# Summing the products of a state-space scan in pairs on GpSimd before TensorE sums over the states

## What is computed

```python
def step(state, inp):
    u, dlt, Bs, Cs = inp
    dA = jnp.exp(dlt.reshape(b, NC, DPG)[..., None] * A_g)
    du = (dlt * u).reshape(b, NC, DPG)
    state = dA * state + du[..., None] * Bs[:, :, None, :]
    y = jnp.einsum('bgdn,bgn->bgd', state, Cs).reshape(b, D_INNER)
    return (state, y)
_, ys = jax.lax.scan(step, init, (u_t, d_t, B_t, C_t))
```

## Time and profile before

| | |
|---|---|
| median of 3 runs | 2097.96 us (2095.51 to 2100.2) |
| the profiled execution | 2099.33 us, its span 2097.5 us |
| PE busy | 1651.5 us, 79% |
| DVE busy | 1770.0 us, 84% |
| ACT busy | 1035.9 us, 49% |
| POOL busy | 913.8 us, 44% |
| mean granted TensorE clock | 0.899 |

### The profile page before, as it was taken

How to read it: one execution, slowest core, us unless ns; L and a number is a source line. 1 busy time by engine, 2 the same in 40 slices (tenths; PEclk the granted TensorE clock), 3 DMA queues, 4 the chain that set the end, 5 groups by cost and what they waited for, 6 DMA issues and landing times. The chain is left out here.

```text
span 2097.5 us, 22567 instructions
## 1 busy us (share of the span) xinstructions
PE 1651.5 (79%) x5875; PEld 725.3 (35%) x5948; DVE 1770.0 (84%) x3142; ACT 1035.9 (49%) x1745; POOL 913.8 (44%) x676
## 2 busy tenths in 40 slices
PE   3375577778996889868997799878997899779856
PEld 1122123232452335322452335332452335234324
DVE  6577899989879998979989998999989987987830
ACT  3247444825555454735556355734547344734312
POOL 0101534454437434554346434464346544665510
PEclk9977699979997999979997899979997899999978
DMA  4100222222222222222231222222222223223300
GB/s 108 46 0 21 72 79 89 92 69 77 75 92 65 85 71 86 85 67 78 74 101 65 81 76 76 96 75 72 76 96 71 76 85 106 86 99 113 110 10 11
DMA packets 94601, 157.95 MB, mean 75 GB/s; under 512 B 10940, under 2 KB 23660, under 8 KB 94468
## 3 DMA queue, kind: packets, MB, share of 16 engines
q1 hardware_dynamic: 94468, 156.43, 22.9%
HBM read 143.83 MB, written 12.58 MB: 75 GB/s over the span
## 5 line engine op out<-in xcount | busy, mean ns | idle before, releaser
L1226 POOL TENSOR_TENSOR prod<-state,c_all 128x512 f32<-128x512 f32 x512 | 669.6, 1312 | 706.8 <-DVE state L1203 644.0
L1203 DVE TENSOR_TENSOR_SCAN state<-decay,ps_b 128x512 f32<-128x512 f32 x512 | 619.7, 1210 | 9.7 <-issue 0.4
L750 PE MATMUL ps_y<-prod,idf 128*128 128x512 f32 x1024 | 610.6, 689 | 4.8 <-DVE u L1216 3.6
L1210 DVE TENSOR_TENSOR ps_b<-du,ps_b 128x512 f32<-128x512 f32 x512 | 347.7, 679 | 87.3 <-PE ps_b L743 86.8
L919 ACT ACTIVATE decay<-delta,a_neg 128x512 f32<-128x512 f32 x512 | 359.3, 719 | 32.3 <-DVE state L1203 29.3
L743 PE MATMUL ps_b<-b_rows,sel_b 48*128 48x512 bf16 x512 | 209.9, 411 | 155.0 <-DVE state L1203 152.7
L750 PEld LDWEIGHTS ps_y<-prod,idf 128*128 128x128 f32 x1024 | 183.8, 207 | 136.3 <-issue 109.9
L743 PEld LDWEIGHTS ps_b<-b_rows,sel_b 48*128 48x128 bf16 x512 | 47.8, 94 | 467.3 <-DVE state L1203 332.5
L619 PE MATMUL ps_x<-xT,w 128*128 128x512 bf16 (+1 forms) x391 | 132.0, 422 | 80.1 <-DVE arena_l L1095 65.6
L826 ACT ACTIVATE arena_l<-ps_x 128x512 f32<-128x512 f32 (+1 forms) x104 | 61.8, 594 | 190.8 <-PE ps_x L619 189.7
L535 PE MATMUL ps_x<-hT,win 128*128 128x512 bf16 (+1 forms) x455 | 135.6, 441 | 21.4 <-DVE arena_b L1171 16.6
(11 more groups left out here) (230 smaller groups left out, 2422.2 us busy)
## 6 DMA issues: line engine op xcount, KB each, us to landing
c_all<-c_rows SPq DMA_DIRECT2D x512, 256.0 KB
c_rows<-arena_l SPq DMA_DIRECT2D x32, 256.0 KB
out<-arena_b SPq DMA_DIRECT2D x8, 512.0 KB
x_in<-in_base SPq DMA_DIRECT2D x8, 256.0 KB
c_all<-in_winT SPq DMA_DIRECT2D x1, 1280.0 KB, 7.5
arena_b<-in_w_fc SPq DMA_DIRECT2D x1, 1024.0 KB, 5.7
arena_b<-in_w_proj SPq DMA_DIRECT2D x1, 1024.0 KB, 5.0
w<-in_w1T SPq DMA_DIRECT2D x1, 792.0 KB, 5.9
```

What stands on the lines that cost most here:

```text
L750: nc.tensor.matmul(ps_y[:], idf[:], prod[:, n % NP, :], start=(n % NST == 0), stop=(n % NST == NST - 1)).then_inc(reduced, 1)
L1203: nc.vector.tensor_tensor_scan(state[:, n % NS, :], decay[:, n % NDA, :], ps_b[:, n % NDB, :], 0.0, ALU.mult, ALU.add).then_inc(scanned, 1)
L1210: nc.vector.tensor_tensor(ps_b[:, j % NDB, :], du[:, slot(s, ct), :], ps_b[:, j % NDB, :], ALU.mult).then_inc(driven, 1)
L1226: nc.gpsimd.tensor_tensor(prod[:, n % NP, :], state[:, n % NS, :], c_all[:, n % NC, :], ALU.mult).then_inc(multiplied, 1)
```

## The change

POOL, after an odd product n, waits for its own product and adds it into the even one before it (new line L1228; the products are L1224 there). A new semaphore `paired` goes up by 2 with each add. PE makes one matmul for a pair instead of one for each product (L752 there), in the slot of the odd one (n + 3), and raises `reduced` by 2. `sums_at` goes. The even product now waits for the matmul of the pair four and three before it, the odd one for the add of that pair. In all 512 sums on PE become 256, and POOL gets 256 adds of 128 x 512 f32, all operands in SBUF.

```diff
             if part == 2:
-                for n in sums_at(j):
-                    if n % NST == 0:
-                        wait(eng, y_taken, s.count(PER, n))
-                    eng.wait_ge(multiplied, s.count(PER, n + 1))
-                    nc.tensor.matmul(ps_y[:], idf[:], prod[:, n % NP, :], start=(n % NST == 0),
-                                     stop=(n % NST == NST - 1)).then_inc(reduced, 1)
-
-        def sums_at(j):
-
-            n = j - 3
-            if not 0 <= n < PER or n % NST == 0:
-                return []
-            return [n - 1, n] if n % NST == 1 else [n]
+                n = j - 3
+                if 0 <= n < PER and n % 2 == 1:
+                    if n % NST == 1:
+                        wait(eng, y_taken, s.count(PER, n - 1))
+                    eng.wait_ge(paired, s.count(PER, n + 1))
+                    nc.tensor.matmul(ps_y[:], idf[:], prod[:, (n - 1) % NP, :], start=(n % NST == 1),
+                                     stop=(n % NST == NST - 1)).then_inc(reduced, 2)
...
                 eng.wait_ge(c_spread[n % 8], s.count(2 * PER, 16 * (n // 8 + 1)))
-                wait(eng, reduced, s.count(PER, n + 1 - NP))
+                if n % 2 == 0:
+                    wait(eng, reduced, s.count(PER, n + 2 - NP))
+                else:
+                    wait(eng, paired, s.count(PER, n + 1 - NP))
                 eng.wait_ge(scanned, s.count(PER, n + 1))
                 nc.gpsimd.tensor_tensor(prod[:, n % NP, :], state[:, n % NS, :], c_all[:, n % NC, :],
                                         ALU.mult).then_inc(multiplied, 1)
+                if n % 2 == 1:
+                    eng.wait_ge(multiplied, s.count(PER, n + 1))
+                    nc.gpsimd.tensor_tensor(prod[:, (n - 1) % NP, :], prod[:, (n - 1) % NP, :], prod[:, n % NP, :],
+                                            ALU.add).then_inc(paired, 2)
```

More of the change, by code:

```diff
@@ L442, in sandwich @@
         multiplied = sem("multiplied")
+        paired = sem("paired")
         reduced = sem("reduced")
```

## The result

The changed kernel takes **2125.4 us** (median of 4 runs, 2123.85 to 2129.3), the one before 2098.07 us beside it. The ratio is 1.0132, with a 95% interval of 1.0117 to 1.0146: slower by 28 us, where 14 us less was forecast. The time lies almost on rival A's, but as the runs show, not by A's sum.

The account below looks back on a forecast made before the run. The prediction took DVE to bound most of a sequence and PE some stretches. Its terms, -61 + 41 + 3 + 3 = -14 us, gave 2084 us, with a range of 2054 to 2126.

Parts of the forecast that it names:

- rival A: DVE stands still longer than PE's relief is worth: 82 us uncovered, +5 for late roots, -61; 2124 us, chance 0.33.
- What bounds the kernel: DVE nearest to full, 1578 of 1746 us busy; PE the bound in some stretches of each sequence.
- term 1: Half of PE's sums go: 0.53 of DVE's 115.6 us of waits at L1210 and the norm comes back, -61 us.
- term 3: Later POOL results delay DVE by +3 us (0 to 20); PE's wait for the add counted as hidden.
- term 2: POOL's 256 adds make DVE instructions with SBUF operands stand still: 58 us, of which +41 us remains after cover.
- term 4: With less work PE may be granted a lower clock, delaying first matmuls of a burst: +3 us (0 to 15).
- made it a rival: Rival B: relief and standing still cancel, or the longest PE waits stand behind other lines' matmuls; 2098 us, chance 0.14.
- L1216 unchanged: DVE's 28.3 us of waits at L1216 for a block's last sums stay, within 10 us over eight ends; counted as 0.
- step that hides an add behind the product: PE's sum waits for POOL's product and add, 2.6 us, but its slot comes 3.8 us later at the shortest: hidden.
- the 0.88 that I had given as a mark: Sign against term 4: a mean PE clock well under 0.88 would break it.
- C's large form: POOL late in middle sequences too, 0.5 us for each of 200 pairs: about 2190 us; chance 0.05 with other slower outcomes.

Follow-up runs that it names:

- relief_selected: Kernel before with only 70 of its sums removed, for selected pairs of products, and no adds (those odd products not summed): 2064.0 us, ratio 0.9841 to the kernel before.
- relief: Changed kernel with half the sums but without the adds on POOL (odd products not summed): 2061.5 us, ratio 0.9836 to the kernel before.
- adds_all_sums: Changed kernel with its adds but 512 sum matmuls on PE again: 2156.8 us, ratio 1.0286 to the kernel before.
- small_pow: Changed kernel with each add on POOL replaced by a power of 128x6, all waits kept: 2076.8 us, ratio 0.9909 to the kernel before.
- tail_pow: Changed kernel with only the adds of states 52 to 63 replaced by a power of 128x6: 2114.9 us, ratio 1.0088 to the kernel before.

## Why the prediction was wrong, by its steps

**What bounds the kernel: right.** DVE bounds most of a sequence, PE two stretches of it and the last feed-forward.

The forecast was 42 us too low (-14 against +28). By the runs, 27 of them are term 1, 12 term 3 and 6 term 2, less the 3 of term 4, whose size is not measured apart: it is inside the relief as the runs show it.

**Term 1, the relief (-61, measured -34): the term that was most mis-sized, and the step that failed.** The stretches were the right ones, but the share 0.53 of 115.6 us was carried over to all sequences from half of the sums' time in a window. *relief_selected* shows that the sums of the stretches where PE is the bound are worth as much as all. In *relief* the two waits fell from 115.6 to 74.3 us, a share of 0.36, and DVE became 8 us more busy (1770.0 to 1778.4), which I had not priced; together a share of 0.29 came back. Part of the base could not shrink: a wait of 4.1 us in each of the second to sixth sequences stands in every one of these kernels at its old length, behind projections and the Gram matrix with hardly a sum among them (in the fourth sequence of the kernel before, DVE waits from 1061.3 to 1065.4). I had seen that long waits might be of this kind and made it a rival instead of looking at each and taking it off the base. The one of 4.4 us in the earlier trace rows, by chance, was of the other kind: it is 3.1 us in *relief*.

**L1216 unchanged: within its bound, but not nothing.** 25.9 us in *relief*, 36.6 in the changed kernel, against 28.3. The 10 us bound held; yet the 11 us between the two are most of what POOL's lateness costs, and the prediction's step that hides an add behind the product did not hold at the ends.

**Term 2, standing still (+58 before cover, +41 after; measured +47): right in size, not in place.** The gross size was right: DVE's busy time rose by 61. The 60 us of *adds_all_sums* are terms 2 and 3 together, for which I had 44; what is the adds' operands alone is the 47 us between *small_pow* and the changed kernel, whose DVE is 65 us more busy. By this pair of runs about 0.3 of it was covered, as I had said, but luck has a part in that: it was not covered in the PE-bound stretch where I had looked for it. In states 36 to 47 of the fourth sequence DVE is 36.0 us busy without adds and 38.4 with them, and the stretch is 42.6 and 44.3 us long (*relief*, then the changed kernel):

```profile
1046.50:1089.10 42.60, 40.72 (x212) 23.96 (x211) 35.97 (x78) 23.05 (x40) 17.23 (x14) 1.00 0.31 104
```

```profile
1069.10:1113.40 44.30, 40.02 (x209) 23.30 (x207) 38.44 (x78) 23.31 (x40) 26.16 (x21) 1.00 0.32 102
```

Of 2.4 us only 0.7 were covered, and over the same states of the first seven sequences 1.3 of 12.9 us (241.7 to 254.6 us busy, 284.0 to 295.6 long). In states 24 to 35 it is 4.5 of 6.2 (241.7 to 247.9, 263.7 to 265.4). A likely reason, not shown, is that DVE waits for PE in a few steps and the adds collide in others; a mean over a stretch does not say that they meet. By the Trainium skill (SBUF — State Buffer, "Who interferes with whom") where the two contend for their shared ports the second to issue blocks until the first is done; the cast above agrees, which ends with POOL's `du`. So does the power, which hardly reads SBUF and costs 47 us less.

**Term 3, waits on POOL (+3, measured +15): mis-sized.** Right that DVE does not wait for POOL itself: no such wait is among the long ones. Wrong in what lateness does: *small_pow* costs 15 us over *relief*, and *tail_pow* puts 19 at the ends of the sequences. DVE waits there for PE, whose last sums wait for POOL, and its short instructions meet products that come later. I looked for waits of DVE for POOL, took the path over PE as hidden unless POOL is behind, gave that case no price, and did not ask what the delayed instructions would collide with. That POOL has much to do in just this place was open to see in any window there (states 56 to 63: 27.6 of 40.8 us before the change, 0.68, against 0.49 over the iterations).

**Term 4, the clock (+3): size open.** The direction was right and larger than thought, 0.899 to 0.815, past the 0.88 that I had given as a mark. PE's busy time fell by only 102 us (some 113 with the missing records) for 305 us of sums: the spread of B went from 411 to 454 ns, a sum's instruction from 689 to 810. Yet *relief* at 0.832 and *relief_selected* at 0.896 take the same time. The 186 further sums gain 9 us in states 24 to 35, and 7 us are lost in states 0 to 15; whether it is the lower clock that takes them was not separated.

**The rivals.** A had the right sign and time, and the right place for what is not covered, with both its figures too large: 82 for 47 of standing still (60 with the lateness, for which it had 5), and 61 for 34. That the difference is the same is luck. C's large form did not come. Chances of 0.48 against 0.38 said that this was near even; the forecast took the wrong side of it, most of all by the size of term 1, and the result lies 0.6 us inside the range's high end.

## What to carry to other kernels

When work is to be moved off an engine, list the waits that end on it one by one, with the removed work that stands ahead of each, and count only those; here 70 of 256 removed sums were worth as much as all. When work is added to GpSimd beside a busy VectorE, price it by place: 0.6 us for an add at the ends of the sequences, where GpSimd has other work queued and VectorE both runs short SBUF-only instructions and soon needs the last result; nothing in the last sequence, where VectorE works from PSUM. Follow the lateness through the third engine too: here VectorE waited for TensorE, which waited for GpSimd. Then apply the change only in the places where it pays.

## What was not expected of the hardware

Taking 305 us of matmuls away freed only 132 us of PE (1651.5 to 1519.6 in *relief*, some 143 with the missing records). The granted clock fell from 0.90 to 0.83, and much of what stayed ran longer: a matmul of the sums 793 ns instead of 689, one of the spread of B 444 instead of 411. And a GpSimd instruction of 1.36 us (128x6, a power), with which DVE is less busy over the whole kernel than without it (1766.1 against 1778.4 us), still cost 0.4 us each at the sequences' ends, by moving others: the last sums came later, and a cast of 0.18 us was 1.24 us long more often.
